# Two MoE layers around attention on one core: the one-hot arrays of the slot table laid out in the natural order of the experts

## What is computed

```python
x = x + 0.5 * ffn(layernorm(x))
x = x + attention(layernorm(x))
x = x + 0.5 * ffn(layernorm(x))
```

```python
scores = sqrt(softplus(h @ gate_w.T))
_, topk_idx = top_k(scores + bias, 6)
eid = topk_idx.reshape(-1)
pos = cumsum(one_hot(eid, 32), axis=0) - 1       # the place of a token in its expert's list
pos = take_along_axis(pos, eid[:, None], axis=1)[:, 0]
valid = pos < 192
xb = zeros((32, 193, 512)).at[eid, where(valid, pos, 192)].set(repeat(h, 6, axis=0))
g, u = xb @ w_gate, xb @ w_up                    # per expert
yb = (silu(g) * u) @ w_down
routed = sum over the 6 picks of yb[eid, pos] * weight
shared = clip(silu(h @ sg.T) * (h @ su.T), -10, 10) @ sd.T
out = routed + shared
```

## Time and profile before

| | us |
|---|---|
| median of 3 runs | 1890.83 |
| lowest and highest of them | 1889.51 and 1900.25 |
| the profiled execution | 1892.66 |
| its span, from first to last instruction | 1890.9 |

### The profile page before, as it was taken

One profiled execution on the slowest core, in us unless ns is written; L12 is line 12 of the kernel. 1 busy time (PEld: TensorE's weight loads), 2 busy tenths in 40 slices (PEclk: granted clock), 3 DMA queues, 4 the chain that ended last, 5 costly groups with the idle time before them and its releaser, 6 DMA issues. The chain is left out here.

```text
span 1890.9 us, 28327 instructions
## 1 busy us (share of the span) xinstructions
PE 1557.8 (82%) x8626; PEld 1268.8 (67%) x8628; DVE 1248.8 (66%) x2561; ACT 975.5 (52%) x2062; POOL 652.1 (34%) x581
## 2 busy tenths in 40 slices
PE   4995867999993889889987997995997666999995
PEld 3774656887773767666776776674775556877774
DVE  5666776777772766585676658564666676777773
ACT  3334045777773555464555546452333144777774
POOL 3000164565552432152233225220000163655553
PEclk9997988999997889989998999898997887999998
DMA  6344306999994101100110111013344315889994
GB/s 215 137 155 171 105 7 202 268 260 261 263 265 87 45 18 51 46 23 34 45 56 12 40 53 32 34 34 111 137 148 152 111 34 172 258 259 264 269 259 90
DMA packets 87198, 244.96 MB, mean 130 GB/s; under 512 B 17648, under 2 KB 18608, under 8 KB 78672
## 3 DMA queue, kind: packets, MB, share of 16 engines
q1 hardware_dynamic: 64592, 192.12, 29.6%
q0 software_dynamic: 22528, 51.92, 13.0%
HBM read 175.25 MB, written 68.76 MB: 129 GB/s over the span
## 5 line engine op out<-in xcount | busy, mean ns | idle before, releaser
L1059 DVE TENSOR_TENSOR e_w_lo<-e_raw,e_w_hi 128x1024 fp32r<-128x1024 f32 x192 | 233.9, 1219 | 108.7 <-ACT e_w_hi L983 108.4
L983 ACT ACTIVATE e_w_hi<-e_raw 128x1024 fp32r<-128x1024 f32 x192 | 202.5, 1056 | 29.7 <-PEq L552 16.6
L1605 POOL TENSOR_SCALAR t_prob<-t_prob,t_inv 128x128 f32<-128x128 f32 (+7 forms) x128 | 96.1, 751 | 291.4 <-DVE t_inv L1492 291.4
L1138 PE MATMUL e_ps_gate<-e_xt,e_w_hi 128*128 128x384 f32 x512 | 163.0, 381 | 32.6 <-DVE e_w_lo L1059 32.5
L1497 DVE TENSOR_TENSOR t_pt<-a_bank,t_pt 128x512 fp32r<-128x512 f32 x144 | 95.6, 687 | 96.0 <-ACT t_pt L1356 95.2
L935 POOL DMA_INDIRECT e_xg<-htab,e_gather_idx x128 | 136.7, 1068 | 62.3 <-issue 43.0
L1138 PE MATMUL e_ps_up<-e_xt,e_w_hi 128*128 128x384 f32 x512 | 151.6, 360 | 0.0
L1349 ACT ACTIVATE t_prob<-a_wide,t_neg_max,a_q_scale 128x128 f32<-128x128 f32 (+7 forms) x128 | 106.5, 832 | 69.9 <-DVE t_neg_max L1486 69.8
L1356 ACT ACTIVATE t_pt<-a_bank 128x512 fp32r<-128x512 f32 x144 | 81.7, 596 | 117.2 <-PE a_bank L1661 116.8
L946 POOL DMA_INDIRECT x_after_ffn<-e_y,e_add_idx x64 | 103.6, 1619 | 109.1 <-DMA x_after_ffn<-e_y,e_add_idx 86.3
L946 POOL DMA_INDIRECT out<-e_y,e_add_idx x64 | 100.9, 1576 | 112.8 <-DMA out<-e_y,e_add_idx 90.4
(11 more groups left out here) (327 smaller groups left out, 4698.9 us busy)
## 6 DMA issues: line engine op xcount, KB each, us to landing
e_raw<-in_w_experts SPq DMA_DIRECT2D x64, 1536.0 KB, 7.9
htab<-d_h SPq DMA_DIRECT2D x16, 1024.0 KB, 4.2
d_x<-in_x SPq DMA_DIRECT2D x16, 512.0 KB, 4.9
q_x<-x_after_ffn SPq DMA_DIRECT2D x32, 256.0 KB, 2.7
t_res<-x_after_ffn SPq DMA_DIRECT2D x32, 256.0 KB, 2.6
x_after_attention<-t_res SPq DMA_DIRECT2D x32, 256.0 KB, 2.1
d_x<-x_after_attention SPq DMA_DIRECT2D x16, 512.0 KB, 5.3
x_after_ffn<-d_y SPq DMA_DIRECT2D x5, 1024.0 KB, 7.3
```

What stands on the lines that cost most here:

```text
L983: act.activation(w_hi[u][:, cols], raw[u][:, cols], ACT.Copy).then_inc(hi_ready, 1)
L1059: dve.tensor_tensor(w_lo[u][:, cols], raw[u][:, cols], w_hi[u][:, cols].bitcast(F32), ALU.subtract).then_inc(lo_ready, 1)
L1138: pe.matmul(out, w[0][:, c, cols], xt[u][:, c, :, :], start=c == 0, stop=False)
L1605: pool.tensor_scalar(prob[:, i % RING, 0:width(i)], prob[:, i % RING, 0:width(i)], inv[:, u:u + 1], 1.0, ALU.mult, ALU.mult).then_inc(p_re ...
```

## The change

The one-hot arrays `hot_a`, `part_a` and `tile_a` are kept as 12 x 32 experts in the natural order, as `hot_b` always was, and no longer as 4 groups x 12 x 8. DVE then writes `hot_a` from one unbroken array of constants. PE picks its group out of the whole array: no longer eight neighbouring experts, but experts g, g + 4, g + 8, ..., so that both sides of the table matmuls are read at a step of 4 elements. In the last matmuls the columns are read in another order, expert within the group first and group last, which gives `slots` the same columns as before. Everything between keeps its shape, and each engine's sequence of instructions, their number and their semaphores are the same in both kernels.

The access patterns as the built program has them, in elements ([step, count] from the outer to the inner), are:

| operand | before | after |
|---|---|---|
| `slot_a` read by DVE | [8, 4] [0, 12] [1, 8] | [0, 12] [1, 32] |
| `iota_a` read by DVE | [8, 4] [32, 12] [1, 8] | [1, 384] |
| `hot_a` written by DVE, read by ACT and POOL | [1, 384] | [1, 384] |
| `tile_a`, `part_a`, stationary side | [1, 96] | [4, 96] |
| `hot_b`, moving side | [32, 16] [1, 8] | [4, 128] |
| `by_group` (fp32), moving side of the last matmuls | [48, 2] [96, 4] [1, 8] | [48, 2] [1, 8] [96, 4] |

```diff
--- before.py
+++ after.py
@@ -500,9 +500,9 @@
         tile_id = sb("r_tile_id", [P, NT], F32)
         diag = sb("r_diag", [SA * EG, SB_, EG], F32)
         dump = sb("r_dump", [HALF, 1], F32)
-        hot_a = [sb(f"r_hot_a{u}_", [P, GE, SA, EG], BF16) for u in range(HOTS)]
-        part_a = [sb(f"r_part_a{u}_", [P, GE, SA, EG], BF16) for u in range(HOTS)]
-        tile_a = [sb(f"r_tile_a{u}_", [P, GE, SA, EG], BF16) for u in range(HOTS)]
+        hot_a = [sb(f"r_hot_a{u}_", [P, SA, E], BF16) for u in range(HOTS)]
+        part_a = [sb(f"r_part_a{u}_", [P, SA, E], BF16) for u in range(HOTS)]
+        tile_a = [sb(f"r_tile_a{u}_", [P, SA, E], BF16) for u in range(HOTS)]
         hot_b = [sb(f"r_hot_b{u}_", [P, SB_, E], BF16) for u in range(HOTS)]
         picked = sb("r_picked", [SA * EG, GE, SB_, EG], F32)
         table = sb("r_table", [SA * EG, GE, SB_], F32)
@@ -611,7 +611,7 @@
                     for u in range(HOTS):
                         act.wait_ge(hots, HOTS * i + u + 1)
                         act.wait_ge(tabbed, HOTS * i + u + 1)
-                        act.activation(tile_a[u][:, :, :, :], hot_a[u][:, :, :, :], ACT.Copy,
+                        act.activation(tile_a[u][:, :, :], hot_a[u][:, :, :], ACT.Copy,
                                        scale=tile_id[:, bass.ds(HOTS * i + u, 1)]).then_inc(ida, 1)
 
             @block.gpsimd
@@ -639,7 +639,7 @@
                         pool.wait_ge(hots, HOTS * i + u + 1)
                         pool.wait_ge(tabbed, HOTS * i + u + 1)
                         pool.sem_inc(seen, 1)
-                        pool.tensor_scalar(part_a[u][:, :, :, :], hot_a[u][:, :, :, :], part_id[:, :], 1.0,
+                        pool.tensor_scalar(part_a[u][:, :, :], hot_a[u][:, :, :], part_id[:, :], 1.0,
                                            ALU.mult, ALU.mult).then_inc(idt, 1)
 
             @block.vector
@@ -756,11 +756,8 @@
                     for u in range(HOTS):
                         t = HOTS * i + u
                         dve.wait_ge(tabbed, HOTS * i + u + 1)
-                        dve.tensor_tensor(hot_a[u][:, :, :, :],
-                                          slot_a[:, bass.ds(t, 1), :].rearrange("p o (g e) -> p g o e", g=GE)
-                                          .to_broadcast([P, GE, SA, EG]),
-                                          iota_a[:, :, :].rearrange("p s (g e) -> p g s e", g=GE),
-                                          ALU.is_equal).then_inc(hots, 1)
+                        dve.tensor_tensor(hot_a[u][:, :, :], slot_a[:, bass.ds(t, 1), :].to_broadcast([P, SA, E]),
+                                          iota_a[:, :, :], ALU.is_equal).then_inc(hots, 1)
                         dve.tensor_tensor(hot_b[u][:, :, :], slot_b[:, bass.ds(t, 1), :].to_broadcast([P, SB_, E]),
                                           iota_b[:, :, :], ALU.is_equal).then_inc(hotb, 1)
                 dve.wait_ge(tabbed, NT + HOTS)
@@ -850,8 +847,8 @@
                         pe.matmul(ps_tab[0:SA * EG, :], no_slots[:, :], hot_b[0][:, :, :].rearrange("p s e -> p (s e)"),
                                   start=True, stop=False)
                     for g in range(GE):
-                        of_group = lambda t: t[:, g, :, :].rearrange("p s e -> p (s e)")
-                        b_of_group = hot_b[u][:, :, g * EG:(g + 1) * EG]
+                        of_group = lambda t: t[:, :, :].rearrange("p s (j g) -> p g (s j)", g=GE)[:, g, :]
+                        b_of_group = hot_b[u][:, :, :].rearrange("p s (j g) -> p g (s j)", g=GE)[:, g, :]
                         out = ps_tab[0:SA * EG, g * EG * SB_:(g + 1) * EG * SB_]
                         pe.matmul(out, of_group(tile_a[u]), b_of_group, start=False, stop=False)
                         got = pe.matmul(out, of_group(part_a[u]), b_of_group, start=False, stop=last and g == GE - 1)
@@ -870,7 +867,7 @@
                 pe.wait_ge(grouped, 1)
                 for at in range(SA // 2):
                     got = pe.matmul(ps_cum[0][0:HALF, 0:2 * E], to_slot[:, at, :],
-                                    by_group[:, :, :, :].rearrange("p g (h a) e -> p h g a e", h=2)[:, :, :, at, :],
+                                    by_group[:, :, :, :].rearrange("p g (h a) e -> p h e a g", h=2)[:, :, :, at, :],
                                     start=at == 0, stop=at == SA // 2 - 1)
                 got.then_inc(turned, 1)
```

## The result

| us | before | after |
|---|---|---|
| median of 20 runs each | 1892.42 | 1898.81 |
| lowest to highest | 1888.24 to 1900.25 | 1892.92 to 1904.80 |
| the profiled execution, its span | 1892.66, 1890.9 | 1899.88, 1898.1 |

The ratio is 1.0029, with a 95% interval of 1.0019 to 1.0039. Times 1892.4 that is 5.5 us slower, 3.6 to 7.4. The median after, 1898.81 us, is inside the forecast range (1886 to 1900), and the ratio is within the 1% that was given 91 in 100. But the interval leaves out 1: it is a real loss, and the forecast had none.

What follows compares the result with a forecast made beforehand. The prediction took VectorE and GpSimd, at 0.912 us a tile, to bound the slot-table loop. Its four terms summed 0 + 0 + 0 + 0, so it forecast the median of before, 1891 us, range 1886 to 1900.

Steps and rivals of the forecast that it cites:

- The bound before: Slot-table loop of each FFN layer: VectorE and GpSimd together set the pace, 0.912 us a tile.
- `r_hot_a` at 0 us: VectorE's first one-hot instruction in the loop: replacing short runs by longer ones changes its time by 0 us.
- The other end, 38 ns: VectorE's r_hot_a wholly in proportion to its elements: 307 ns instead of 345, a gain of 2.1 us in all.
- ACT and POOL at 0: r_tile_a on ScalarE and r_part_a on GpSimd read and write 384 neighbouring elements in either version: 0 us.
- The table matmuls at 0: TensorE's 256 table matmuls on each of two lines: step 4 has no price, 0.057 us each, 0 us change.
- the first rival: Table matmuls make TensorE the bound: 0.21 us each, +53 us, 1944 us; 6 in 100.
- The text's own sign of being wrong: In the after-trace, table matmul starts over 0.114 us apart and VectorE waiting for TensorE in every tile.
- The high end: Table matmuls: TensorE passes over all 512 elements for 128, 0.21 us each, +26.6 us a layer.
- The case between the ends: Table matmuls at twice 0.057 us: only the first and last bursts show, 0.9 us a layer, 1.8 in all.
- The last matmuls at 0: Last matmuls reading by_group at a column step of 96: 0 us, at most +2.1 us a layer, 4.1 in all.
- DVE and POOL meeting otherwise, or not at all: Two loop rivals: whole instructions exclude each other, 1907 us, 4 in 100; or the meeting goes away, 1874 us, 3 in 100.
- likeliest case: Whole kernel: nothing to see, 1891 us, bounds 1888.7 to 1896.7; 87 in 100.

Runs made afterwards that it cites:

- before_part_dve: Kernel before, with GpSimd out of the loop and its multiply by the partition number done by VectorE: 0.9976 of before.
- dve_alone: Kernel before, with only hot_a in natural order from unbroken constants; ScalarE and GpSimd read runs of 8 and write group order: 1.0006 of before.
- probe: Kernel before, with 16 extra matmuls of each of eleven operand-step forms behind the loop; moving steps 1, 2, 4, 8: 0.056, 0.057, 0.114, 0.227 us a matmul.
- 1/4: Extra matmuls added to the kernel before, stationary side at step 1 and moving side at step 4, in bf16 elements: 0.114 us each at full clock.
- 1/8: Extra matmuls added to the kernel before, stationary side at step 1 and moving side at step 8, in bf16 elements: 0.226 to 0.227 us each.
- probe2: Kernel before, with six strided matmul forms behind the loop, 80 dense matmuls ahead of each; stationary step 4 alone 0.090 us, both sides at 4 0.118.

## Why the prediction was right, and where it wasn't

- *The bound before*, DVE and POOL at 0.912 us a tile: right, shown by `before_part_dve`. So was PE's room, 0.114 us a matmul.
- *`r_hot_a` at 0 us*: right, by `dve_alone` and by 357 ns in the kernel after. The other end, 38 ns, was wrong.
- *ACT and POOL at 0*: right in the rows by tile.
- *The table matmuls at 0*: this is the step that failed. The text took the low end, 0.057 us, because the moving side before already jumps 64 bytes after every 8 elements. That was the wrong likeness: in `probe` runs of 8 behind a jump cost 0.057 us and a step of 4 costs 0.114. The measured 0.118 us lies 0.004 over the limit the text had worked out, so the first rival's mechanism is what happened, at a smaller price: 0.118 us a matmul and not 0.21, 6.0 us in all and not 53. The text's own sign of being wrong, starts over 0.114 us apart, has come true. (Where it writes "the second rival" of an error in the count of elements, it means this first one.) The high end, all 512 elements passed over, was also wrong; a step of 32 costs that, a step of 4 half of it.
- *The case between the ends*, "twice today's 0.057", was sized at 0.9 us a layer and came out at 2.9. Its first and last burst are right, 8 x 0.06 = 0.49 us each. Missed were three things in the first layer: 25 tiles of 0.03 us beyond the limit, 0.8 us; that in the kernel before the ring refills at 0.61 us a tile while POOL lags (251.16, 251.77, 252.37), which a busy PE doesn't allow, 0.7 us; and that PE comes to the last tile 2.50 us behind the start of its `r_hot_a`, where it was 2.02, 0.5 us.
- *The last matmuls at 0*: right. They take 2.18 us in the changed kernel against 2.06, but the granted clock there is 0.50 against 0.66 before, and in `dve_alone`, with the old column order and a clock of 0.50, it is 2.18 too. A column step of 96 shows no price at that clock; at 1.00 it wasn't measured. The windows of the kernel after and of `dve_alone`:

```profile
284.00:288.00 4.00, 2.18 (x12) 1.99 (x12) 2.75 (x8) 0.00 (x0) 0.00 (x0) 0.50 0.20 76
285.50:287.90 2.40, 2.18 (x12) 1.99 (x12) 1.32 (x4) 0.00 (x0) 0.00 (x0) 0.50 0.11 43
```

- *DVE and POOL meeting otherwise, or not at all*: neither happened. The meeting moved from one instruction to the other at the same total.
- *The rule of the Trainium skill* (SBUF — State Buffer, "Door 1: The DMA port swizzle"), by which a step of 8 bytes with two elements to a line is free: the measurement decides against it at 2.4 GHz, where it doubles the matmul's time, and nearly for it at 1.2 GHz, 0.117 against 0.105 us.

The range and the "within 1%" held although the sum was wrong, and that is in part luck. The loop is small, 60 us of 1892 for both layers, and the measured price of a matmul lies just over the limit. The result, 1898.81, is already over the 1896.7 that the text gave as the upper bound of its likeliest case, and only the allowance for the spread of single runs still holds it. Of the 7.8 us between 1891 and the result, 1.6 are the kernel before itself, whose median of 20 runs is 1892.42.

## What to carry to other kernels

Before an operand of TensorE is read at a stride, count how many of its columns lie in 16 bytes. In these runs, at the full clock and with 128 bf16 columns on the moving side, four were free, two doubled the time of a matmul and one quadrupled it. The stationary side had nearly the same price for a column, and the greater of the two showed. Then divide the pace of the loop by its number of matmuls; here the answer was 0.114 us against 0.118, so the edit moved the bound from one engine to another and cost 0.3%. Tidying a pattern whose short runs cost nothing, as `dve_alone` shows of this one, gives nothing; what paid was to take apart the meeting of two engines, 0.30 us a tile.

## What was not expected of the hardware

- A strided matmul costs a time and not cycles: 1/4 takes 0.114 us at 2.4 GHz and 0.117 at 1.2.
- The granted clock can fall though PE's records leave no gap: behind 16 matmuls of the form 1/8, which filled 3.6 us, it was 0.50 in `probe`, and 0.73 on the mean of the 80 dense matmuls that follow them in the first layer of `probe2`. It isn't so each time: in the second layer of `probe2` the same 80 take 4.48 us in place of 6.00, as at the full clock.
- VectorE's multiply of 384 bf16 elements by a number for each partition takes 0.23 us from start to start, against 0.58 us at least on GpSimd, and without slowing its neighbours.
- A cast with permuted output, 1024 elements from int32 to bf16, takes 2.44 us on VectorE against 0.69 in order.
